# Attention of a post-norm decoder layer: the score is issued ahead of the maximum in each pair

## The reference

```python
qkv = x @ qkv_w + qkv_b                       # b n 3 H D
attn = jnp.einsum('bnhd,bmhd->bhnm', q, k) * scale
attn = jax.nn.softmax(attn, axis=-1)
out = jnp.einsum('bhnm,bmhd->bnhd', attn, v).reshape(b, n, c)
out = out @ proj_w + proj_b
x = _layernorm(x + out, axis=-1)
```

## Time and profile before

| | |
|---|---|
| median of 3 runs | 3653.32 us |
| lowest, highest | 3651.91, 3653.96 us |
| span of the profiled execution, first to last instruction | 3644.6 us |
| TensorE busy in that span | 94% |
| VectorE, ScalarE, GpSimd busy | 69%, 46%, 55% |
| attention stage, about | 100 to 2170 us |

### The profile page before, as it was taken

One profiled execution on the slowest core, in us unless ns is written; L12 is line 12 of the kernel. 1 busy time (PEld: TensorE's weight loads), 2 busy tenths in 40 slices (PEclk: granted clock), 3 DMA queues, 4 the chain that ended last, 5 costly groups with the idle time before them and its releaser, 6 DMA issues. The chain is left out here.

```text
span 3644.6 us, 50074 instructions
## 1 busy us (share of the span) xinstructions
PE 3423.0 (94%) x18021; PEld 2227.0 (61%) x18021; DVE 2510.0 (69%) x4512; ACT 1672.6 (46%) x3043; POOL 1995.2 (55%) x1008
## 2 busy tenths in 40 slices
PE   7999999999999999999999987999959899999996
PEld 5545455455455555455454435877739789988885
DVE  5777777777777777777777735889834765566667
ACT  2455555555555555555555553444312333233332
POOL 2688888888888888888898950011110101110112
PEclk9999999999999999999999998999969999999998
DMA  6322221321312312213120022132132333323332
GB/s 223 103 56 65 86 62 62 93 67 61 97 50 73 97 50 85 73 50 106 56 64 24 15 93 66 58 121 81 53 119 81 113 113 104 116 89 114 117 128 99
DMA packets 190278, 308.49 MB, mean 85 GB/s; under 512 B 25514, under 2 KB 72234, under 8 KB 190011
## 3 DMA queue, kind: packets, MB, share of 16 engines
q1 hardware_dynamic: 166970, 243.82, 21.8%
q0 software_dynamic: 14592, 44.32, 3.5%
q10 hardware_dynamic: 8448, 16.78, 1.3%
HBM read 195.66 MB, written 61.33 MB: 71 GB/s over the span
## 5 line engine op out<-in xcount | busy, mean ns | idle before, releaser
L511 DVE TENSOR_REDUCE sa_part_max<-sa_mx 128x1 f32<-128x512 f32 x2048 | 1282.4, 680 | 539.8 <-PE sa_mx L625 536.0
L466 ACT ACTIVATE sa_prob<-sa_sc 128x512 f32<-128x512 f32 x2010 | 1101.3, 595 | 803.7 <-PE sa_sc L692 764.4
L268 POOL TENSOR_TENSOR sa_quad_sum<-sa_quad_sum,sa_prob 128x1024 f32<-128x1024 f32 x500 | 1174.6, 2382 | 6.3 <-ACT sa_prob L466 6.3
L268 POOL TENSOR_TENSOR sa_quad_sum<-sa_prob 128x1024 f32<-128x1024 f32 x250 | 588.2, 2372 | 266.9 <-ACT sa_prob L466 266.9
L2055 PE MATMUL ex_h<-ex_xT,ex_w 128*128 128x384 f32 (+2 forms) x2688 | 463.9, 328 | 52.0 <-issue 24.4
L625 PE MATMUL sa_mx<-sa_k_even,sa_q_stack 96*128 96x512 f32 x1024 | 490.8, 483 | 17.2 <-DVE sa_part_max L511 7.5
L625 PE MATMUL sa_mx<-sa_k_odd,sa_q_stack 96*128 96x512 f32 x1024 | 476.6, 465 | 10.0 <-DVE sa_part_max L511 8.6
L2055 PEld LDWEIGHTS ex_h<-ex_xT,ex_w 128*128 128x128 f32 x2688 | 445.3, 194 | 64.8 <-issue 32.6
L692 PE MATMUL sa_sc<-sa_q_stack,sa_k_even 98*128 98x512 f32 x1024 | 427.1, 417 | 0.0
L2066 PE MATMUL ex_acc<-ex_w,ex_hT 128*128 128x512 f32 x1719 | 415.6, 392 | 1.9 <-DVE ex_hT L1994 1.6
L692 PE MATMUL sa_sc<-sa_q_stack,sa_k_odd 98*128 98x512 f32 x986 | 415.5, 423 | 1.6 <-ACT sa_prob L466 1.6
(11 more groups left out here) (229 smaller groups left out, 3776.8 us busy)
## 6 DMA issues: line engine op xcount, KB each, us to landing
ex_w_in<-in_L_ffn_w_dram SPq DMA_DIRECT2D x130, 512.0 KB, 4.1
sa_xT<-xT SPq DMA_DIRECT2D x57, 1024.0 KB, 5.1
sa_q_stack<-sa_hilo SPq DMA_DIRECT2D x372, 64.0 KB, 2.0
rows<-sa_empty SPq DMA_DIRECT2D x48, 257.0 KB, 3.7
ex_rows<-rows POOLq DMA_DIRECT2D x8, 1542.0 KB, 7.7
sa_k_odd<-sa_hilo SPq DMA_DIRECT2D x192, 64.0 KB, 2.0
ex_xg<-rows POOLq DMA_DIRECT2D x48, 256.0 KB
sa_k_even<-sa_hilo SPq DMA_DIRECT2D x168, 64.0 KB, 2.0
```

Source lines behind the costliest of these rows:

```text
L268: pool.tensor_tensor(quad_sum[:, i % 2, heads, :], so_far, prob[:, k, heads, :], ALU.add).then_inc(quad_ready, 1)
L466: act.activation(prob[:, kt % 4, j, :], score_bank(n)[:, :], ACT.Exp, scale=SCALE).then_inc(prob_ready, 1)
L511: dve.reduce_max(part_max[:, q, j, k:k + 1], mx[n % 3][:, :], AX_X).then_inc(max_read, 1)
```

## The change

In `chunk`, the call of `score` now stands ahead of `max_pass` in each pair. The numbers, the waits inside both and all else are as they were.

```diff
                 for i in range(HG):
                     n = (g + 1) * NMAX + LEAD + kt * PER_STEP + i
+                    score(g, kt, i)
                     if n < CHUNKS * NMAX:
                         max_pass(n, n % NMAX, n // NMAX)
-                    score(g, kt, i)
                     if g < LAST or kt <= 2:
                         if i == 1 and kt % 2 == 0:
                             burst(g, kt)
```

## The result

The changed kernel takes 3658.51 us (median of 13 runs, 3651.66 to 3663.04), the kernel before beside it 3651.91 us (13 runs). The ratio is 1.0017, with a 95% interval of 1.0009 to 1.0025: 6.6 us slower, at the upper edge of "within 0.2%". A second series gave 1.0016 (1.0007 to 1.0025). The forecast was 0.95 us slower, so the direction and the range held, and the size was short by some 5.7 us. The span of the profiled execution is 3653.7 us, against 3644.6. These two spans can't be compared as the medians can: the profiled execution of the changed kernel took 3655.41 us, 1.7 more than its span, and 1.7 to 1.8 us is what launch and end take in every execution on record. The 8.7 us that I called launch and end in the forecast were therefore, at most, 1.8 us of it, and the rest, some 7 us, is by how much the profiled execution of the kernel before was quicker than the median.

What follows compares the result with a forecast made beforehand. It took TensorE's order of work, with short waits in it, as the bound. Late chunk starts (+1.65 us) and the last chunks (-0.7) gave +0.95 on 3653.32, so 3654.3 us, range 3648 to 3662.

Steps and rivals of the forecast that it cites:

- What stays: Within the attention steps, scores' waits on ScalarE and maxima's on VectorE's reductions were to stay unchanged: change 0.
- the neighbours: Maxima ahead of fillers and scores behind them were taken to cost 0, within plus or minus 3.3 us.
- (a): Shift transposes T after step 13's third pair: wait 0.12 us, covered by later maxima's VectorE waits; cost 0, uncovered 3.7 us.
- (b): Projection part P ending step 4: its wait for VectorE's L505 grows a slot (0.235 us), covered in step 5; cost 0.
- my signs: Profile signs to check afterwards, such as P in step 4 waiting about 0.7 us and T about 0.12.
- (c): Chunk boundary: seven starts waiting for shift rows behind SP's k moves each come a slot later, 7 x 0.235 = +1.65 us.
- theory W: From the experiments: a weight load carries one wait; a second is an instruction costing about 0.06 us ahead of ScalarE-released scores.
- The step that failed: For the whole swap of about 1900 pairs: nothing added or removed, no wait with another count, unchanged waits priced at 0.
- The gain in the last chunks: Last three chunks with maxima: earlier scores feed GpSimd sooner, so T comes earlier; 0 to -1.4 us, taken as -0.7.
- The lead over GpSimd: Step 13: L522's start ahead of GpSimd's addition was to fall from 0.79 to 0.32 us, staying above 0.
- the rival: Step 13's lead vanishes, L522 ends with GpSimd's addition: some 2.4 us a chunk, 28 times 67 us, 3721 us; chance 0.11.

Runs made afterwards that it cites:

- experiment 1: Changed kernel with step 13's wait for the stacks moved from ahead of the first score to between that score and its maximum: 3654.75 us, ratio 1.0005.
- experiment 12: The changed kernel measured once more, unaltered, for the spread of its late starts and last chunks: 3659.71 us, ratio 1.0016.
- experiment 6: Kernel before with a long-fulfilled wait added ahead of the third maximum of each odd step: 3653.05 us, ratio 1.0003.
- experiment 7: Kernel before with step 13's first reduction taken ahead of L520 and L522 on VectorE, so the shift comes about 0.6 us later: 3660.94 us, ratio 1.0025.
- experiment 5: Kernel before with a long-fulfilled wait added ahead of the third score of each odd step: 3661.22 us, ratio 1.0019.
- experiment 4: Changed kernel with stacks and shift-row waits each set between a score and its maximum, six of twelve k moves issued behind the shift DMAs: 3648.86 us, ratio 0.9995.
- the late shift: Changed kernel with step 13's first reduction taken ahead of L520 and L522 on VectorE, the shift about 0.6 us later: 3761.45 us, ratio 1.0302.

## Why the prediction was right, and what was mis-sized

**What stays.** Right in time. The waits of scores on ScalarE within a step are the same (0.25 us above a slot for the third score of step 1 before, 0.25 to 0.26 after), and the neighbours cost what I took: a maximum ahead of a burst is 0.547 us from end to end as the score was, and a score behind one 0.430 as the maximum was (0.429). My lines that the scores' waits stand near 238 us and the maxima's near 114 were wrong (186.3 and 32.9), without a cost in time that shows.

**(a) The transposes.** The cost of 0 was right, the wait of 0.12 us was not. L522 ends at 1011.94 and the load of T starts at 1011.99, held by it, but only the loader waits: the first transpose ends 0.11 us behind the matmul ahead of it in both kernels, so TensorE never waited and no cover was needed. Behind T the scores take over what VectorE no longer holds: the second score of step 14 stands 0.23 us above a slot (0.03 before), the two maxima of that step 0.02 together (0.22 before).

**(b) P at the end of step 4.** Right. Its idle time went from 0.22 us to 0.45, one slot more (the "about 0.7" among my signs was a slip, since 0.22 + 0.235 is 0.46), and the fourth maximum of step 5 gives it back: it stands 0.56 us above a slot instead of 0.83 (chunk 14, changed kernel):

```profile
1041.73 1.10 PE L616 MATMUL sa_misc<-sa_xT,sa_wq 128*128 128x512 f32 x2 [0.45 <-DVE sa_hilo L505]
...
1044.33 0.42 PE L692 MATMUL sa_sc<-sa_q_stack,sa_k_odd 98*128 98x512 f32 x1
...
1045.04 0.49 PE L625 MATMUL sa_mx<-sa_k_odd,sa_q_stack 96*128 96x512 f32 x1 [0.30 <-DVE sa_part_max L511]
```

**(c) The late chunk starts.** The mechanism was right, the size was not: 7 x 0.235 = 1.65 us in the forecast. In the changed kernel the seven starts stand 0.94 us above a slot on average, in experiments 1 and 12 1.02 and 0.93: together 0.96 us. With the maximum first they stand at 0.64 in the kernel before, and at 0.54 and 0.54 in experiments 6 and 7: together 0.57 (experiment 5, whose own waits move every chunk, has 0.49). The difference is 0.39 us a start, 2.7 us for seven. Of the 0.39, 0.235 is the slot and 0.06 is theory W (the shift's wait and ScalarE's stand in front of the same score). The remaining 0.1 is not settled: SP's twelve moves take 7.5 to 8.7 us from one chunk to the next, and 8.01 us on average with the score first against 7.87 with the maximum first, a difference smaller than their spread.

**The step that failed** is the sentence that nothing is added and no wait has another count, with the pricing of all that stays at 0. The counts are the same, but the place of two waits changed, from a maximum with slack to a score without. I had looked at what is queued behind each wait, not at what the wait itself takes to issue. Priced by experiments 1 and 4, it is 0.06 us at step 13 and 0.07 at the chunk's start; the third score of step 13 comes 0.03 us later besides, and there are small changes the other way. From the end of a chunk's first pair to that of the next one, a second, third and fourth chunk of a unit took 65.07, 65.08 and 64.35 us before (medians), 65.24, 65.24 and 64.45 in the changed kernel and 65.22, 65.21 and 64.43 in experiment 12: 0.12 to 0.14 us more, in 31 chunks 3.7 to 4.3 us. My forecast called itself wrong if the chunks' length changed by more than 0.1 us. By that sign it was wrong, and the range held because it had room for terms that I had not named.

**The gain in the last chunks,** -0.7 us, is there in the waits and not in the time. T's three waits sum to 9.4 to 10.0 us in the five traces with the maximum first and `top` in SBUF, and to 8.6 to 8.7 in the six with the score first, some 1.2 us less. But from chunk 28 to the last value product the same five take 246.2 to 249.9 us, and those with the score first 247.2 to 250.1 (243.3 with the late shift): the time at 1.2 GHz in this stretch lies between 17.1 and 37.5 us in these traces and differs by more than the gain. I had also read L520 alone there; in the kernel before L522 is held once too (2.27 us in chunk 28).

Together: 2.7 us for the late starts and 3.7 to 4.3 for the ordinary loss of all chunks, less 0.4 that is in both (7 x 0.06), is 6.0 to 6.6 us for the 6.6 measured, 0.7 less if the last chunks gain. Between chunk 1 and 28, where 27 chunks count, the same sum is 27 x 0.12 to 0.14 + 2.7 - 0.4 = 5.5 to 6.1 us; the traces show 6.2 for the changed kernel and 4.9 for experiment 12. A stretch of 3.4 us at 1.2 GHz stands behind the longest late start of the changed kernel (1.55 us above a slot) and of experiment 1 (1.72), and not behind that of 12 (1.51); at half the clock it costs up to 1.7 us, which is the size of that gap. Three traces don't say what decides it. The sum is made of small differences in single traces, so that it meets the medians this well is in part luck.

**The lead over GpSimd** was forecast to fall from 0.79 to 0.32 us, in chunk 8 from 0.60 to 0.13. It fell to 0.38 and 0.19 (that score of step 13 comes 0.06 late, and GpSimd with it). The order of these two was right, and the price of the rival was too low: 67 us forecast, about 100 measured once the lead was gone. The 2.4 us a chunk were right for the wait (T waits 2.5 us longer); the term that I left out is the clock behind it.

## What to carry to other kernels

When two instructions of a queue are swapped, follow the waits in front of them too: a wait that costs nothing ahead of an instruction with slack costs its own issue time ahead of one that another engine releases. When two engines meet on a shared resource, write down the lead between them; it appears in no busy share and in no list of waits, and half of it can vanish in an edit that measures as no change. If the operand can lie elsewhere, take it off the shared resource rather than tune the lead.

## What the runs showed of the hardware

- In these programs a weight load carried one wait. With two, one was an instruction of 51 ns in front of it, and delayed a load that another engine released by 0.06 to 0.07 us; ahead of a maximum with slack it cost nothing measurable.
- An instruction of VectorE with two SBUF operands that started 0.14 us behind an addition of GpSimd lasted until that was over (2.23 us for 0.18), 28 times out of 28; with one operand in PSUM it took 0.18 us beside the same addition.
- A wait of TensorE of some 3 us cost more than itself: with three such waits gone, 9.9 us in all, the granted clock of the last chunks rose from 0.93 to 0.98, and 249.4 us became 229.7. With 2.5 us more of waiting in each chunk, 27 stretches at 1.2 GHz came between chunk 1 and 28 where there had been one.
